# Who rounds the quantised context: the rounding of sixteen tiles moves from VectorE to GpSimd

## What is computed

```python
def fake_quant(x, scale, zp):
    q = jnp.clip(jnp.round(x / s + z), QMIN, QMAX)      # 0 to 255
    return (q - z) * s

x = x + tanh(g_xattn[0]) * matmul(fake_quant(layernorm(x)), fake_quant(ctx_4096))
x = x + tanh(g_ffn[0])   * (quant_per_token(layernorm(x)) @ dequantize(W_int).T + bias)
x = x + tanh(g_xattn[1]) * attention(layernorm(x), ctx_4096, Wq, Wk, Wv, Wo)
x = x + tanh(g_ffn[1])   * (layernorm(x) @ dequantize_fp4(weight_packed, scales).T)
```

## Time and profile before

| | us |
|---|---|
| median of 3 runs | 879.41 |
| lowest and highest | 879.01, 881.24 |
| the profiled execution | 881.43 |
| its span on the core | 879.6 |
| PE busy | 832.4 (95%) |
| DVE busy | 587.4 (67%) |
| POOL busy | 532.9 (61%) |
| ACT busy | 449.7 (51%) |
| the sixteen roundings on DVE, L1003 | 11.8 |
| POOL's sixteen affines, L492, and clamps, L494 | 27.2 and 22.5 |

### The profile page before, as it was taken

One profiled execution on the slowest core, in us unless ns is written; L12 is line 12 of the kernel. 1 busy time (PEld: TensorE's weight loads), 2 busy tenths in 40 slices (PEclk: granted clock), 3 DMA queues, 4 the chain that ended last, 5 costly groups with the idle time before them and its releaser, 6 DMA issues.

```text
span 879.6 us, 13992 instructions
## 1 busy us (share of the span) xinstructions
PE 832.4 (95%) x4458; PEld 327.5 (37%) x4458; DVE 587.4 (67%) x850; ACT 449.7 (51%) x741; POOL 532.9 (61%) x235
## 2 busy tenths in 40 slices
PE   7889899899999999999999999999999989999998
PEld 6566554344444422222222222222222213444443
DVE  5886748988387557788777787778788711355622
ACT  4545445655322156676767676777676673111200
POOL 5435328966343337788878888888888787121200
PEclk9989999999999989999999999999999999999999
DMA  8899953437995215445355345455445243132242
GB/s 272 239 262 255 193 175 90 102 85 125 249 235 150 69 51 129 94 85 129 88 124 117 87 102 122 92 123 123 92 92 127 54 91 76 27 67 48 49 137 77
DMA packets 120822, 107.79 MB, mean 123 GB/s; under 512 B 85325, under 2 KB 105805, under 8 KB 116685
## 3 DMA queue, kind: packets, MB, share of 16 engines
q1 hardware_dynamic: 115120, 71.59, 32.1%
q0 software_dynamic: 4608, 33.56, 18.9%
q10 hardware_dynamic: 1052, 2.10, 0.9%
HBM read 41.55 MB, written 12.58 MB: 62 GB/s over the span
## 4 chain that ended last, share of the span: by engine, by line
PE 65%; DVE 11%; issue 10%; DVEq 4%; POOLq 3%; DMA 2%; POOL 2%; ACT 1%; SPq 0%; ACTq 0%
PE sbank L1617 11%; PE sbank L1626 11%; PE mpair L1557 9%; DVE mx L1298 5%; DVEq L931 3%; PE sbank L1435 3%; PE sbank L1437 3%; PE sbank L1436 3%; PE sbank L1695 3%; PE sbank L1710 3%; PE sbank L1712 3%; PE sbank L1697 3%; PE sbank L1699 3%; POOLq L493 3%; POOL xT_lo L494 2%
## 5 line engine op out<-in xcount | busy, mean ns | idle before, releaser
L1298 DVE TENSOR_REDUCE mx<-mpair 128x1 f32<-128x1024 f32 x256 | 301.0, 1215 | 86.2 <-PE mpair L1557 86.0
L873 ACT ACTIVATE regC<-sbank 128x512 f32<-128x512 f32 x512 | 279.7, 595 | 125.4 <-PE sbank L1617 124.7
L1617 PE MATMUL sbank<-regD 98*128 98x512 f16 x512 | 179.2, 387 | 11.4 <-DMA regD<-mT 5.4
L599 POOL TENSOR_TENSOR wraw<-regC 128x2048 f32<-128x2048 f32 x32 | 145.2, 4538 | 26.4 <-ACT regC L873 15.6
L1557 PE MATMUL mpair<-regD 96*128 96x512 f16 x512 | 156.6, 383 | 3.1 <-DVE mT L1308 2.8
L1626 PE MATMUL sbank<-regC,regD 128*32 128x512 f32 x1024 | 137.2, 608 | 1.0 <-ACT regC L873 1.0
L1617 PEld LDWEIGHTS sbank<-regD 98*128 98x128 f16 x512 | 46.4, 97 | 202.9 <-ACT regC L873 162.7
L599 POOL TENSOR_TENSOR regD<-regC 128x2048 f32<-128x2048 f32 x16 | 72.9, 4559 | 25.8 <-ACT regC L873 25.7
L599 POOL TENSOR_TENSOR tail<-regC 128x2048 f32<-128x2048 f32 x16 | 76.7, 4795 | 0.8 <-ACT regC L873 0.8
L1557 PEld LDWEIGHTS mpair<-regD 96*128 96x128 f16 x512 | 49.3, 99 | 55.1 <-DVE mT L1308 9.9
L492 POOL TENSOR_SCALAR xT_lo<-xT_lo,sc 128x1024 f32<-128x1024 f32 x16 | 27.2, 1703 | 49.4 <-DVE X L983 36.3
(11 more groups left out here) (183 smaller groups left out, 1244.4 us busy)
## 6 DMA issues: line engine op xcount, KB each, us to landing
regD<-wraw POOLq DMA_DIRECT2D x16, 1024.0 KB, 7.0
tail<-wraw POOLq DMA_DIRECT2D x16, 1024.0 KB, 7.0
xT_lo<-in_ctx SPq DMA_DIRECT2D x16, 512.0 KB, 5.3
wraw<-in_L_ffn_W_int SPq DMA_DIRECT2D x8, 512.0 KB, 4.9
X<-in_x SPq DMA_DIRECT2D x4, 1024.0 KB, 6.9
wraw<-in_L_xattn_Wq SPq DMA_DIRECT2D x8, 512.0 KB, 3.8
wraw<-in_L_xattn_Wo SPq DMA_DIRECT2D x8, 512.0 KB, 4.4
regD<-q_hi_scratch SPq DMA_DIRECT2D x32, 128.0 KB, 2.4
```

Of the source, the lines that this page charges most:

```text
L599: nc.gpsimd.tensor_tensor(p_sum[pr if pr < 3 else 1][:, :, :], probs[:, (2 * pr) % 4, :, :], probs[:, (2 * pr) % 4 + 1, :, :], ALU.add).th ...
L873: nc.scalar.activation(probs[:, kt % 4, h, :], bank[4 + h % 2], ACT.Exp, scale=SCALE).then_inc(s["exp_ok"], 1)
L1298: v.tensor_reduce(mx[m][:, bass.ds(n, 1)] if par is not None else mx[m][:, n:n + 1], slot[:, :, :], AX.XY, ALU.max).then_inc(s["mx_red"], 1)
L1617: pe.matmul(bank[4 + h % 2], kst[par][0:98, kt * P:(kt + 1) * P], qst[par][0:98, h * 512:(h + 1) * 512], start=True, stop=True).then_inc(s ...
```

## The change

POOL's `ctx_affine(u)` gets a second drain and a third operation, the rounding that DVE did, with the same numbers and the same output. It counts `cq_done` itself. DVE's `ctx_round` and its sixteen calls go, and with them the semaphore `cq_pool`. Nothing else is changed; SyncE and PE wait for the same counts of `cq_done`.

```diff
             def ctx_affine(u):
...
                 nc.gpsimd.tensor_scalar(cx[:, u % TB, :], cx[:, u % TB, :], IS2, Z2, ALU.mult, ALU.add)
                 pool.drain()
-                nc.gpsimd.tensor_scalar(cx[:, u % TB, :], cx[:, u % TB, :], 255.0, 0.0, ALU.min,
-                                        ALU.max).then_inc(s["cq_pool"], 1)
+                nc.gpsimd.tensor_scalar(cx[:, u % TB, :], cx[:, u % TB, :], 255.0, 0.0, ALU.min, ALU.max)
+                pool.drain()
+                nc.gpsimd.tensor_scalar(r2[:, u, :], cx[:, u % TB, :], MAGIC, MAGIC + ZC, ALU.add,
+                                        ALU.subtract).then_inc(s["cq_done"], 1)
...
-            def ctx_round(u):
-                dve.wait_ge(s["cq_pool"], u + 1)
-
-                v.tensor_scalar(r2[:, u, :], cx[:, u % TB, :], MAGIC, MAGIC + ZC, ALU.add,
-                                ALU.subtract).then_inc(s["cq_done"], 1)
...
             turned_low(1, 2)
-            ctx_round(0)
             turned_low(2, 4)
-            ctx_round(1)
             turned_low(3, 6)
             wkv_low(0)
-            ctx_round(2)
             wkv_low(1)
             turned_low(4, 6)
             dve.wait_ge(s["wsc_in"], 16)
             wd_scale(0)
-            ctx_round(3)
...
                 ctx_low(u + 1)
-                ctx_round(u)
                 wd_low(2 * c)
                 wd_scale(2 * c + 1)
...
                 ctx_low(u + 2)
-                ctx_round(u + 1)
                 ln1_round(2 * c)
                 ctx_low(u + 3)
-                ctx_round(u + 2)
                 k_low(c, 0)
                 ln1_round(2 * c + 1)
                 wd_low(2 * c + 1)
                 wd_scale(2 * c + 2)
-                ctx_round(u + 3)
                 k_low(c, 1)
```

More of the change, by code:

```diff
@@ L184, in build @@
             wkv_hi wkv_lo
-            ctx_tr ct_hi ct_lo ctx_hi ctx_lo cth0 cth1 ctl0 ctl1 cq_pool cq_done
+            ctx_tr ct_hi ct_lo ctx_hi ctx_lo cth0 cth1 ctl0 ctl1 cq_done
             wd_prod wd_tr wd_hi_ok wd_lo_ok
```

## The result

| | before | changed |
|---|---|---|
| median of 5 runs, us | 879.38 | 888.28 |
| lowest and highest | 877.76, 881.24 | 886.42, 890.44 |
| ratio of the times | | 1.0093, interval 1.0068 to 1.0117 |

The change makes the kernel 8.9 us slower. The forecast was +1.5 us, and its range ended at 883.4. (Of the kernels further down, two additions, two additions in the last four tiles, and tiles 8 to 11 each had one slow execution, at 904.56, 4711.67 and 1074.00 us, which is left out of their medians and ratios.) The reason stands in one row of the page of the changed kernel; its columns are busy us, mean ns of one, and the idle time before.

A forecast was written before the change was run, and what follows sets the result against it. No compute engine is full; the chain of waits through `wd_scale(6)` on DVE to PE at 104.76 us was taken to bound it. Places A, B and C, 0.5 + 0 + 1.0 = +1.5, on 879.4 gave 880.9 us, range 877.9 to 883.4.

The forecast's parts named there:

- Place B: SyncE's context buffer reloads after `cq_done`: rounding ready 1 us early for `load_ctx(11)`, early loads go out sooner; 0.
- the cover: At `load_ctx(11)`: rounding ends 1 us before SyncE gets there at 51.36; lost if a rounding takes 2.13, costing about 1.
- third rival: POOL becomes late: roundings at 2.13 us delay `wd_scale(1)`, `ctx_low(6)` and `load_ctx(11)`; +4.1, 883.5 us, chance 0.13.
- Place A: 8 to 40 us: POOL busy longer, so `wd_scale(1)` waits for its operation under way; +0.5, bounds 0 and +1.1.
- Place C: 95.9 to 104.8 us, on the chain: `wd_scale(6)` waits for a whole POOL rounding; +1.0, bounds -0.0 and +2.0.
- two races: POOL starts before DVE twice: affine 0.1 us ahead of `ln1_round(4)`, rounding under 0.1 us ahead of `wd_scale(6)`.
- step 4: Near 103.5 us: POOL's rounding is first by under 0.1 us, so `wd_scale(6)` waits for it, 0.96 us.
- step 3: From 97.8 us: POOL's clamp, rounding and affine make `ln1_round(5)` end at 102.4, before 102.38; nothing is won.
- Step 1: Near 96 us: POOL's affine begins 0.1 earlier, so `ln1_round(4)` waits and ends at about 97.8, not 97.16.
- second rival: DVE's saving arrives: PE resumes 1.0 us earlier, full clock gives 1.7 more; 876.7 us, chance 0.08.

The follow-up runs named there:

- two additions: The changed kernel with POOL's rounding written as add and add of a negative constant instead of add and subtract: 887.35 us, ratio 1.0094.
- two additions in the last four tiles: POOL rounds only tiles 12 to 15, by add and add, DVE the rest as in the kernel before: 879.46 us against 879.88, ratio 0.9996.
- tiles 8 to 11: POOL rounds only tiles 8 to 11, by add and subtract, DVE the rest as in the kernel before: 881.31 us, ratio 1.0021.
- the cheap kernel: Changed kernel, all sixteen roundings on POOL: affine adds the large number, clamp moved up, third operation multiplies by 1 and adds: 877.73 us, ratio 0.9978 to before.
- the first twelve tiles alone: POOL rounds tiles 0 to 11 by add and subtract, DVE tiles 12 to 15 as in the kernel before: 889.96 us, ratio 1.0124.
- the first four slow: Changed kernel, all roundings on POOL, add and subtract in tiles 0 to 3, multiply-add pairs in tiles 4 to 15: 884.70 us, ratio 1.0049 to before.
- the last four alone: POOL rounds only tiles 12 to 15, by add and subtract, DVE the rest as in the kernel before: 879.59 us against 879.28, ratio 1.0007.
- The run at 2.23 us for a rounding: Changed kernel with each POOL rounding as two multiply-add operations and a drain between: 882.95 us, ratio 1.0030 to before.
- the two kernels that are the kernel before up to tile 15: Kernel before with extra tensor-scalar operations on POOL behind tile 15, seven in one, further pairs in the other: 879.87 and 880.86 us, one execution each.
- the kernel with the first seven extra operations: Kernel before plus seven POOL operations behind tile 15 (add-subtract, minimum-maximum, multiply-multiply, f16 or f32 output): 879.87 us in one execution against 879.28.

## Why the prediction was wrong, point by point

**The price of a rounding on POOL is the step that failed.** The prediction took 1.04 us, from L512, with 2.13 from L514 as the upper bound. It measured 3.63 where nothing holds it up. The doubt was laid on the f16 output, which costs nothing. It was the pair of operations, add and subtract, that no row of POOL before had: L492 is multiply-add, L494 minimum-maximum, and both are among the cheap ones. The prediction treated "tensor-scalar, one input, 128x1024" as one kind. The range inherited the bound of 2.13 and could not hold the result. The Trainium skill ("GPSIMD Engine Reference"), which it quoted, calls VectorE about 2x faster for elementwise work under "Key points", and under "Engine selection" ties the 2x to operations with two inputs and puts one input at roughly line rate. It pointed the right way, but the rows here differ from both: one input, 3.63 to 0.68, a factor of 5.3. By the cheap kernel against the changed one the price is worth ten us.

**Place B, the buffers, was given 0.** The cover was 1 us at `load_ctx(11)`, and "if the cover goes" it was to cost about 1. With 6.16 us for a tile, that load goes out 12.6 us late. The prediction also put the tight place too far back. The delay grows from the first load that waits for a rounding: `load_ctx(4)` goes at 16.30 where it went at 14.52, `load_ctx(5)` at 22.47 (18.02 before), and `load_ctx(6)` and the W_int load behind it at 32.02 and 32.39, 8.4 us later than before (23.58 and 23.95), where the text had said that the early loads go out sooner. With the price as forecast they do: in the cheap kernel at 20.87 and 21.24. This term holds the loss, by the runs with the first twelve tiles alone (all of it), with the first four slow (about half, measured against the kernel before) and with the last four alone (none).

**The third rival, POOL late, was nearest.** It named `wd_scale(1)` and the load of tile 11, and the point from which it decides, 1.6 us for a rounding, lies below what was measured. But it had `wd_scale(1)` held up by an operation on POOL, where in the changed kernel it waits 2.72 us for its slice and then takes its plain 1.23, and only 1.0 of its 4.1 us came from a late load. The run at 2.23 us for a rounding gave 882.95, near the rival's 883.5, yet `load_ctx(11)` went out there at 56.20, 4.8 us later than before, not 1.0. The agreement of the sum is in part luck.

**Place A** was forecast at +0.5, by `wd_scale(1)` held up. In the cheap kernel `wd_scale(1)` starts at 33.51 and takes 1.22: it isn't held up but starts 0.5 later. The transpose behind it goes at 40.88, where 40.9 was forecast and 40.40 was before. That agreement is luck: in the two kernels that are the kernel before up to tile 15 the transpose goes at 41.53 and 40.31. From the start of `wd_scale(0)` to the transpose the code of before takes 14.60, 14.59 and 14.59 us, the cheap kernel 14.69 (26.19 to 40.88). So behind `wd_scale(0)`, the one that is held up there (2.04 us), place A cost 0.1, not 0.5.

**Place C** was forecast at +1.0 by two races that POOL wins. In the changed kernel neither costs DVE anything: `ln1_round(4)` takes 0.69, and `wd_scale(6)` 1.21, not 2.1, though it begins in the middle of a rounding on POOL (below). The cheap kernel shows both at the price forecast, and there DVE wins both races. (The margin of step 4 did not come from its own steps either: step 3 gives the affine of tile 15 1.05 us, 100.8 to 101.85, where no affine in the rows takes less than 1.19, and that is more than the 0.08 us by which the race was called.) Step 1 failed first. Then `ln1_round(5)` starts at 100.00, not at 101.37, and `wd_scale(6)` comes 0.86 us sooner behind `wd_scale(5)`. That is the second rival, DVE's saving arrives, which had 1.0 us and a chance of 0.08. PE's wait shrinks from 3.35 us to 2.49, near what that rival said (2.35), but the clock does not stay up there, and its further 1.7 us don't come:

```profile
103.53 1.97 PE L1397 MATMUL sbank<-id,wraw 128*128 128x128 f32 x8 [2.49 <-DVE wraw L1006]
```

```profile
103.00:108.00 5.00, 4.47 (x28) 3.94 (x29) 2.46 (x4) 1.85 (x4) 2.43 (x2) 0.66 1.22 181
```

So with the price that the forecast assumed the result would have been about 877.5 (879.4 x 0.9978; 875.9 to 879.0 by the interval), not 880.9. The sign of place C would have been missed at either price: from `wd_scale(5)` to `wd_scale(6)` the move saves 0.86 us with the cheap pairs and as much with add and subtract in the last four tiles, where +1.0 was forecast.

**DVE busy** was to fall by 9 to 10 us, apart from operations that get longer. It fell by 7.0: the sixteen roundings were 11.8, and the low parts, `ln1_round` and `wd_scale` together take 2.1 us more than before. The rest of the difference was not traced.

## What to carry to other kernels

Before an operation moves to GpSimd, find a row of GpSimd with the same pair of operations, not only with the same shape and number of inputs, or run the pair by itself; and where a pair is dear, see whether the arithmetic can be spread over the operations already there, as multiply-add and minimum-maximum. Where an engine's work releases buffers of a ring, look at the first round of the ring: here it carried 6.2 of the 10.1 us, and other loads stand behind it in the same queue. A race that two engines decide by a tenth of a microsecond is no basis for a term of a sum; give it both outcomes. The same code moved by up to 1.2 us at one place from one execution to another, so a term of 0.5 us can't be read from a start time in one trace; the length of a stretch that holds only the place in question was good to 0.01 us here.

## What the runs showed of the hardware that was not expected

- On POOL, a tensor-scalar operation of two steps on 128x1024 f32 takes 1.04 us or 3.63 us by its pair of operations: multiply-multiply, multiply-add, add-multiply and minimum-maximum the one, add-add, add-subtract, subtract-multiply and add-minimum the other (multiply-subtract 4.68, once). On DVE the add-subtract takes 0.69 us.
- Which engine is held up does not follow from whose row begins first. In the cheap kernel POOL's affine begins at 95.70 and DVE's `ln1_round(4)` at 95.84, and POOL is the one that takes 0.55 us more than its 1.19.
- The dear operation does not keep DVE out for its whole length. In the changed kernel POOL rounds tile 14 from 110.31 on:

```profile
110.31 3.63 POOL L496 TENSOR_SCALAR regR<-xT_lo 128x1024 f16<-128x1024 f32 x1 [0.15 <-issue]
```

  `ln1_round(5)`, begun 0.43 us into it, takes 1.15 and ends 1.58 us into it, which is 0.69 behind 0.89. `wd_scale(6)`, begun 2.70 us into it, takes its plain 1.21. The other tiles of the changed kernel read the same: each `ln1_round`, low part or `wd_scale` that began within 0.45 us of the rounding's start ends 0.9 us and its own plain length behind that start, each that began 1.3 us or more behind it takes its plain length. So the rounding held DVE up for about 0.9 us out of 3.63, not for its whole length, as the exclusive lock that the prediction quoted from the Trainium skill ("SBUF — State Buffer", "SBUF: two separate sides") would have it. That fits the last four tiles, whose move cost nothing.
- The same wait of PE was followed by either clock. In the kernel with the last four tiles on POOL, PE waits 2.49 us at this place, as in the cheap one, and the windows view has the clock at full speed behind it:

```profile
104.82 1.09 PE L1419 MATMUL sbank<-id,wraw 128*128 128x128 f32 x8 [2.49 <-DVE wraw L1020]
```

```profile
105.00:110.00 5.00, 5.00 (x47) 4.56 (x47) 1.65 (x3) 1.47 (x3) 4.69 (x3) 1.00 1.10 227
```

  There the addition to X that ends is at 136.24, 1.6 us earlier than before, with `wd_scale(6)` at 103.56, against 103.50. The longer wait too was followed by either: the kernel with the first seven extra operations is the kernel before up to tile 15 and has the same wait of 3.35 us, and where the kernel before had 0.66 behind it, it has full speed:

```profile
105.54 1.09 PE L1426 MATMUL sbank<-id,wraw 128*128 128x128 f32 x8 [3.35 <-DVE wraw L1027]
```

```profile
106.00:111.00 5.00, 5.00 (x48) 4.53 (x47) 2.47 (x5) 1.47 (x3) 4.21 (x2) 1.00 1.12 207
```

  So the clock behind such a wait can't be forecast from its length, as the second rival did. What decides between the two, these runs don't show.
